# Two kinds of attention scores in the two row halves of TensorE, their matmuls interleaved, the causal mask in two 64-row parts

## The reference

```python
x = x + _L0_attn_ref(_layernorm(x), Wqkv, Wout)
    qkv = z @ Wqkv
    attn = einsum('nhqd,nhkd->nhqk', q, k) * 8 ** -0.5
    attn = softmax(where(causal, attn, -inf))
    out = einsum('nhqk,nhkd->nhqd', attn, v) @ Wout
x = x + _L0_ffn_ref(_layernorm(x), ...)     # 8 experts, two of them per token
x = x + _L1_attn_ref(_layernorm(x), ...)    # rotary, one key and value head for all 16 query heads
x = x + _L1_ffn_ref(_layernorm(x), ...)     # blockwise fp4 quantised, gated
```

## Time and profile before

| | |
|---|---|
| runs | 761.79, 761.80, 763.25 us; median 761.8 |
| profiled execution, first to last instruction | 757.7 us |
| PE matmul busy | 660.7 us (87%), 5007 instructions |
| VectorE busy | 514.1 us (68%) |
| ScalarE busy | 342.2 us (45%) |
| GpSimd busy | 151.8 us (20%) |
| mean granted TensorE clock | 0.965 of full |
| chain that ended last | PE 64%, DVE 25%, issue 5%, ACT 3% |

### The profile page before, as it was taken

One profiled execution on the slowest core, in us unless ns is written; L12 is line 12 of the kernel. 1 busy time (PEld: TensorE's weight loads), 2 busy tenths in 40 slices (PEclk: granted clock), 3 DMA queues, 4 the chain that ended last, 5 costly groups with the idle time before them and its releaser, 6 DMA issues.

```text
span 757.7 us, 13009 instructions
## 1 busy us (share of the span) xinstructions
PE 660.7 (87%) x5007; PEld 464.5 (61%) x5007; DVE 514.1 (68%) x1313; ACT 342.2 (45%) x472; POOL 151.8 (20%) x145
## 2 busy tenths in 40 slices
PE   1478889999989899999999998999989899998664
PEld 0333556565655699898998785775555655555443
DVE  6578776777743536658537467777786778666993
ACT  1110566656575444433444432335546455674221
POOL 5301010100011010010021301302203010345764
PEclk9995999999999999999999999999999999999985
DMA  5405876454320000000000200211211211000000
GB/s 152 126 22 147 173 218 132 85 141 75 66 55 14 1 1 1 1 1 1 1 1 1 63 1 12 75 23 28 83 42 27 65 45 35 25 12 1 14 15 28
DMA packets 29325, 38.07 MB, mean 50 GB/s; under 512 B 3719, under 2 KB 23185, under 8 KB 29265
## 3 DMA queue, kind: packets, MB, share of 16 engines
q1 hardware_dynamic: 29265, 37.25, 20.3%
HBM read 26.33 MB, written 10.88 MB: 49 GB/s over the span
## 4 chain that ended last, share of the span: by engine, by line
PE 64%; DVE 25%; issue 5%; ACT 3%; POOL 1%; DMA 0%; POOLq 0%; DVEq 0%; ACTq 0%
PE ps L989 14%; PE ps L486 9%; PE ps L444 7%; DVE mx L663 6%; PE ps L465 6%; PE ps L979 4%; PE ps L512 3%; PE ps L981 3%; PE ps L980 3%; DVE xn L926 3%; PE ps L447 2%; ACT pT L557 1%; PE ps L494 1%; PE ps L469 1%; DVE x L1063 1%
## 5 line engine op out<-in xcount | busy, mean ns | idle before, releaser
L663 DVE TENSOR_REDUCE mx<-ps 128x1 f32<-128x384 f32 (+3 forms) x352 | 215.5, 637 | 72.5 <-PE ps L447 70.4
L557 ACT ACTIVATE pT<-ps 128x1024 f32<-128x1024 f32 x160 | 162.1, 1023 | 86.9 <-PE ps L469 71.9
L1024 ACT ACTIVATE pT<-ps,b1c 128x512 f32<-128x512 f32 x128 | 87.8, 687 | 129.6 <-PE ps L981 128.7
L989 PEld LDWEIGHTS ps<-w_sb,pT 128*128 128x128 f32 x1024 | 132.2, 191 | 11.8 <-issue 1.3
L989 PE MATMUL ps<-w_sb,pT 128*128 128x128 f32 x1024 | 135.5, 275 | 0.0
L447 PE MATMUL ps<-mask_qk,identb 128*128 128x128 bf16 (+2 forms) x352 | 90.2, 256 | 0.0
L444 PE MATMUL ps<-stA 96*128 96x128 bf16 (+3 forms) x256 | 69.6, 332 | 19.2 <-DVE mx L663 14.3
L486 PE MATMUL ps<-pT,vA 128*32 128x512 f32 (+3 forms) x1024 | 77.9, 439 | 0.7 <-ACT pT L557 0.7
L1063 DVE SCALAR_TENSOR_TENSOR x<-ps,comb,x 128x128 f32<-128x128 f32 x128 | 36.0, 344 | 58.4 <-PE ps L989 58.3
L444 PE MATMUL ps<-kA,stA 96*128 96x128 bf16 (+3 forms) x256 | 63.7, 304 | 12.8 <-DVE mx L663 11.6
L979 PE MATMUL ps<-x_hi,w_hi 128*128 128x512 f32 x128 | 62.9, 491 | 1.2 <-DVE w_lo L1045 1.0
(11 more groups left out here) (232 smaller groups left out, 964.1 us busy)
## 6 DMA issues: line engine op xcount, KB each, us to landing
stA<-stack_scratch SPq DMA_DIRECT2D x48, 192.0 KB, 3.4
stB<-stack_scratch SPq DMA_DIRECT2D x48, 192.0 KB, 4.5
stack_scratch<-part SPq DMA_DIRECT2D x12, 384.0 KB, 3.2
w_sb<-in_L_ffn_W_dram SPq DMA_DIRECT2D x16, 256.0 KB, 5.6
stack_scratch<-part SPq DMA_DIRECT2D x12, 256.0 KB, 3.1
stack_scratch<-part SPq DMA_DIRECT2D x12, 128.0 KB, 3.1
x<-in_L_attn_z_dram SPq DMA_DIRECT2D x4, 256.0 KB, 4.4
out_dram<-x SPq DMA_DIRECT2D x4, 256.0 KB, 2.3
```

The source lines that it names most:

```text
L557: act.activation(dst_, src, ACT.Exp, scale=SCALE).then_inc(a["ex"], 1)
L663: nc.vector.tensor_reduce(mx[:, g % 2, qb, heads[0]:heads[0] + nh], ps[:, S_BANK[n % 2], 0:nh * w].rearrange("p (h k) -> p h k", h=nh), AX ...
L989: last = pe.matmul(ps[:, ST_BANK[1] + m % 2, f * P:(f + 1) * P], hT[:, (m % 2) * FC + c, f * P:(f + 1) * P], w2_sb[:, e, c, :], start=(c = ...
L1024: act.activation(hT[:, (m % 2) * FC + f, :], ps[:, ST_BANK[0] + n % 2, :], ACT.Gelu, bias=b1c[:, e * FC + f:e * FC + f + 1]).then_inc(M["g ...
```

## The change

- S reads partitions 0 to 47, ST partitions 64 to 114 of one stack `st` that replaces `stA` and `stB`. `kA`, the rotary table and the picking columns of layer 1 are made in both places (`KW` = 112 partitions instead of 48), so the key projection has 112 columns.
- No rows are padded, so the clears and the waits on them are gone.
- Each mask matmul (128 rows of identity) becomes two of 64 rows: the first adds the mask's own 64 rows over all 128 columns, the second (`identx`, `mask_x`, which GpSimd makes at the start) adds the other 64 rows to the 64 columns that they touch. S uses the lower half for both, ST the upper.
- Every score and mask matmul is a step of its own, and within a part v the steps of S and ST are merged. Where an attention step is merged with another stage, that merge now counts these finer steps.
- The input loads of the rotary table and the picking columns are six DMAs instead of two.

```diff
+HI = 64
+MR = HI + SR
+KW = HI + SR
+ST_UNITS = [[(j, kb) for kb in (0, 1, 3)] for j in range(HG)] + [[(j, 2) for j in range(HG)]]
+def s_steps(b, g, *units):
+    return [("S", b, g, (u, m)) for u in units for m in range(len(S_UNITS[u][1]) + 2)]
+def st_steps(b, g, u):
+    return [("ST", b, g, (u, m)) for m in range(len(ST_UNITS[u]) + 4)]
...
             for v in range(NV + 1):
-                if s < B:
-                    o.append(("S", s, g, 2 * v))
-                if v < NV and 1 <= s <= B:
-                    o.append(("ST", s - 1, g, v))
-                if v < NV and s < B:
-                    o.append(("S", s, g, 2 * v + 1))
+                plain = s_steps(s, g, *range(2 * v, min(2 * v + 2, NS))) if s < B else []
+                turned_ = st_steps(s - 1, g, v) if v < NV and 1 <= s <= B else []
+                o += merged(plain, turned_)
...
-    o = of("A0", first0[:1]) + setup("QKCOLS") + of("A0", first0[1:2]) + setup("CLEAR")
+    o = of("A0", first0[:1]) + setup("QKCOLS") + of("A0", first0[1:2])
...
-        stA = sb("stA", [KR, 2, 2 * HG, T], BF16)
-        stB = sb("stB", [KR, 2, 2 * HG, T], BF16)
+        st = sb("st", [P, 2, 2 * HG, T], BF16)
...
-                for m, j in enumerate(heads):
-                    h = (g % 2) * HG + j
-                    kk = stA[:, 1, h, :] if layer == 0 else kA[:, b, :]
-                    pe.matmul(ps[:, bank, m * w:(m + 1) * w], stA[:, 0, h, qb * P:w], kk[:, 0:w],
+                if m < nh:
+                    h = (g % 2) * HG + heads[m]
+                    kk = st[0:SR, 1, h, :] if layer == 0 else kA[0:SR, b, :]
+                    pe.matmul(ps[:, bank, m * w:(m + 1) * w], st[0:SR, 0, h, qb * P:w], kk[:, 0:w],
                               start=(m == 0), stop=False)
-                pe.matmul(diagonal, identb[:], mask_qk[:].unsqueeze(1).broadcast_to([P, len(heads), P]),
-                          start=False, stop=True).then_inc(a["sc"], 1)
+                elif m == nh:
+                    pe.matmul(diagonal, identb[0:HI, :], mask_qk[0:HI, :].unsqueeze(1).broadcast_to([HI, nh, P]),
+                              start=False, stop=False)
+                else:
+                    pe.matmul(diagonal[:, :, HI:P], identx[0:HI, :],
+                              mask_x[0:HI, HI:P].unsqueeze(1).broadcast_to([HI, nh, P - HI]),
+                              start=False, stop=True).then_inc(a["sc"], 1)
...
+                    kk = st[HI:MR + 3, 1, h, :] if layer == 0 else kA[HI:MR + 3, b, :]
+                    pe.matmul(o, kk[:, kb * P:(kb + 1) * P], st[HI:MR + 3, 0, h, kb * P:T], start=(at % 512 == 0), stop=False)
...
+                    if not second:
+                        pe.matmul(diagonal, identb[HI:P, :], mask_kq[HI:P, :].unsqueeze(1).broadcast_to([P - HI, nd, P]),
+                                  start=False, stop=False)
+                    else:
+                        last = pe.matmul(diagonal[:, :, 0:HI], identx[HI:P, :],
+                                         mask_x[HI:P, 0:HI].unsqueeze(1).broadcast_to([P - HI, nd, HI]),
+                                         start=False, stop=True)
...
-            if name == "CLEAR":
-                v.memset(stA[:, 1].rearrange("p h t -> p (h t)"), 0.0).then_inc(cleared_a, 1)
...
-            if name == "CLEAR":
-                nc.gpsimd.memset(stB[:].rearrange("p c h t -> p (c h t)"), 0.0).then_inc(cleared_b, 1)
...
-            sp.dma_start(rk[:], rope_k.rearrange("c p t -> p c t")).then_inc(ld_w1, 16)
-            sp.dma_start(pick_sb[:], pick).then_inc(ld_w1, 16)
+            for lo, n in ((0, SR), (SR, HI - SR), (HI, SR)):
+                sp.dma_start(rk[lo:lo + n], rope_k[:, 0:n].rearrange("c p t -> p c t")).then_inc(ld_w1, 16)
+                sp.dma_start(pick_sb[lo:lo + n], pick[0:n]).then_inc(ld_w1, 16)
...
-            nc.vector.memset(stA[:, 0].rearrange("p h t -> p (h t)"), 0.0).then_inc(cleared_a, 1)
...
+            link(nc.gpsimd, nc.gpsimd.memset(identx[:], 0.0))
+            for base in (HI, -HI):
+                link(nc.gpsimd, nc.gpsimd.affine_select(identx[:], identx[:], compare_op=ALU.not_equal, fill=1.0, base=base,
+                                                        pattern=[[-1, P]], channel_multiplier=1))
+            link(nc.gpsimd, nc.gpsimd.memset(mask_x[:], 0.0))
+            link(nc.gpsimd, nc.gpsimd.affine_select(mask_x[:, 0:HI], mask_x[:, 0:HI], compare_op=ALU.is_ge, fill=NEG, base=HI,
+                                                    pattern=[[1, HI]], channel_multiplier=-1))
+            link(nc.gpsimd, nc.gpsimd.affine_select(mask_x[:, HI:P], mask_x[:, HI:P], compare_op=ALU.is_ge, fill=NEG, base=0,
+                                                    pattern=[[-1, HI]], channel_multiplier=1))
```

More of the change, by code:

```diff
@@ L72, with s_last, st_last, merged @@
 NV = HG + 1
+ST_UNITS = [[(j, kb) for kb in (0, 1, 3)] for j in range(HG)] + [[(j, 2) for j in range(HG)]]
[3 more added lines that the diff above has]
+    return [("ST", b, g, (u, m)) for m in range(len(ST_UNITS[u]) + 4)]
+def s_last(step):
+    return step[1] == len(S_UNITS[step[0]][1]) + 1
+def st_last(step):
+    return step[1] == len(ST_UNITS[step[0]]) + 3
+def merged(one, two):
+    at = [((i + 0.5) / len(one), 0, i) for i in range(len(one))] + [((i + 0.5) / len(two), 1, i) for i in range(len(two))]
+    return [(one, two)[w][i] for _, w, i in sorted(at)]
 def attention_order(layer):
@@ L178, in fp4_order @@
     return o + rest(m) + [("DA", n // pairs, n % pairs, 0) for n in (m - 1, m)]
-def merged(one, two):
-    at = [((i + 0.5) / len(one), 0, i) for i in range(len(one))] + [((i + 0.5) / len(two), 1, i) for i in range(len(two))]
-    return [(one, two)[w][i] for _, w, i in sorted(at)]
 def network_order():
@@ L257, in network @@
         mask_kq = sb("mask_kq", [P, P], BF16)
+        identx = sb("identx", [P, P], BF16)
+        mask_x = sb("mask_x", [P, P], BF16)
         ones = sb("ones", [P, P])
@@ L404, in attention_sync @@
             elif name in ("LOADA", "LOADB"):
-                st, ld, used, per = (stA, "loadA", "sc", NS) if name == "LOADA" else (stB, "loadB", "st", NV)
+                lo, ld, used, per = (0, "loadA", "sc", NS) if name == "LOADA" else (HI, "loadB", "st", NV)
                 ws = slice((g % 2) * HG, (g % 2 + 1) * HG)
-                if name == "LOADA" and i == 0 and layer == 0:
-                    sp.wait_ge(cleared_a, 2)
                 if name == "LOADA" and g == 0:
@@ L544, in attention_scalar @@
             if name == "ST":
+                if not st_last(u):
+                    return
+                u = u[0]
                 n = i * NV + u
```

133 lines of the change are left out of this document (68 added, 65 removed).

## The result

The changed kernel takes 795.65 us (median of 4 runs, 793.85 to 797.67) against 761.79 us for the kernel before (4 runs, 760.64 to 763.25): ratio 1.0441, 95% interval 1.0412 to 1.0471. It is 34 us slower, outside the forecast range and with the other sign. Its profiled execution spans 794.5 us (757.7 before), at a mean granted TensorE clock of 0.934 (0.965).

The account below looks back on a forecast made before the run. The prediction took TensorE as the bound, with VectorE 0.9 us behind per group. Its terms summed to -9.4 us on a 757.7 us span, 748.3, plus 4.1 to reach the median: 752.4 us, range 740 to 770.

Parts of the forecast that it names:

- a, head: Start of the kernel: without the clears, normalisations and the first transpose come earlier, -5.6 us.
- b, S alone: Layer 0 with only S: longer masks and more mode changes, partly hidden, +1.2 us (0 to +3).
- Changes of tile: Each change of TensorE's tile size, throughout the kernel, taken as 0.096 us (0 to 0.20).
- c, steps 1 to 3 of layer 0: Layer 0 with S and ST overlapping: twelve groups shorten from 11.27 to about 10.4 us each, -10 us.
- rival 5: TensorE's granted clock drops to 1.2 GHz for 20 us of the steps, 10 us more: 762 us; chance 0.05.
- d, ST alone: Layer 0 with only ST: longer masks and 17 changes, half behind exp, +2.4 us (+1 to +4).
- e, experts with S of layer 1: Expert matmuls land inside S units: 88 added changes and masks, less TensorE idle time, +8 us.
- f, steps 1 to 3 of layer 1: Layer 1 with S and ST overlapping: 0.75 us saved per group over twelve groups, -9 us.
- g, ST alone with fp4: Layer 1's ST alone beside the fp4 stage: masks and 31 changes, a part hidden, +3.6 us.
- Rival 2: The row halves don't overlap, so steps 1 to 3 lengthen in both layers: 796 us; chance 0.10.
- Rival 1: Each of 232 added mode changes costs 0.17 us on the path, not 0.096: 769 us; chance 0.12.
- Rival 3: S waiting for its bank holds up ST, losing half the gain in steps 1 to 3: 762 us; chance 0.10.

Follow-up runs that it names:

- e5: The kernel before, with GpSimd's clear of stB waiting until VectorE's clears of stA are done: 756.02 us, ratio 0.9933.
- e11: The kernel before, with only each mask split into two 64-row matmuls, scores kept at 96 rows: 883.51 us, ratio 1.1605.
- e12: The kernel before, with only the scores cut to 48 and 51 rows, without the zero rows, masks kept single: 884.61 us, ratio 1.1658.
- e4: e2 plus a 64-row, 512-column filler matmul ahead of nine of eleven S units in steps 1 to 3: 776.93 us, ratio 1.0218.
- e8: e4 with the filler also while S is alone in layer 0, and two of them in layer 1: 794.21 us, ratio 1.0438.
- e9: e2 plus a 64-row, 256-column filler matmul ahead of nine of eleven S units in steps 1 to 3: 775.88 us, ratio 1.0197.
- e2: The changed kernel, with S and ST units kept whole where merged with expert or fp4 steps: 784.99 us, ratio 1.0324.
- e3: e2 in the old order, a whole S unit, a whole ST unit, a whole S unit: 781.84 us, ratio 1.0283.
- e10: e9 with its 256-column filler on all 128 rows instead of 64: 793.96 us, ratio 1.0343, with scattered runs.
- e6: The kernel before in its own order, S and ST both in rows 0 to 63, masks in two parts: 856.24 us, ratio 1.1253.
- e1: The kernel before, 96-row stacks and 128-row masks kept, with S and ST matmuls alternating as single steps: 765.11 us, ratio 1.0059.
- e7: e2 with an expert H step and the Y step behind it merged as one block: 793.13 us, ratio 1.0424.

## Why the prediction was wrong, point by point

**a, head (-5.6): right.** Timeline of all engines in the changed kernel:

```profile
7.59 1.11 DVE L938 TENSOR_SCALAR xn<-x,mv,rstd 128x128 f32<-128x128 f32 x4 [1.94 <-POOL rstd L945]
...
8.85 1.09 PE L512 MATMUL ps<-ident,xn 128*128 128x128 f32 x4 [8.85 <-DVE xn L938]
```

The first transpose was at 14.21 and is at 8.85, the first S at 29.2 instead of 34.8: -5.6. e5 shows the clear as the cause, by moving it alone.

**b, S alone (+1.2): too small, +4.8.** TensorE, a score matmul of 512 columns and its mask near the end of this stretch, before and after:

```profile
77.63 0.39 PE L444 MATMUL ps<-stA 96*128 96x512 bf16 x1 [1.07 <-DVE mx L663]
77.85 0.22 PE L447 MATMUL ps<-mask_qk,identb 128*128 128x128 bf16 x1
```

```profile
76.17 0.60 PE L440 MATMUL ps<-st 48*128 48x512 bf16 x1 [0.86 <-DVE mx L680]
76.57 0.31 PE L443 MATMUL ps<-mask_qk,identb 64*128 64x128 bf16 x1
```

0.22 us from start to start before, 0.40 after: after, TensorE is still at half speed here, though the stage row above says 0.99. In both traces the column shows 1.00 up to the first recorded fall, and isn't to be trusted there. The pair of before stands just behind its rise at 76.3: before too had 34.9 of its 44.2 us at half clock, after has all 49.0. The earlier trace rows gave 0.82 for this stage, and I used that only as a warning. e5, with the matmuls of before and 7.4 us more at half clock, takes 1.1 us longer here; at that rate the 14.1 us more are some 2 of the 4.8 (an estimate), and the rest is left to the masks and changes.

**Changes of tile (0.096 us): the price was right (0.10 in e11 and e12).** The Trainium skill (TensorEngine Tiling, Key Properties) says that such a change drains TensorE; the traces agree, with those 0.10 us. What failed is how much of it other work covers. Between the experts the price is the same. TensorE, S and then H in the kernel after:

```profile
482.15 0.32 PE L440 MATMUL ps<-kA,st 48*128 48x384 bf16 x1
482.41 0.50 PE L991 MATMUL ps<-x_hi,w_hi 128*128 128x512 f32 x1
482.75 0.40 PE L992 MATMUL ps<-x_lo,w_hi 128*128 128x512 f32 x1
482.99 0.40 PE L993 MATMUL ps<-x_hi,w_lo 128*128 128x512 f32 x1
483.32 0.23 PE L443 MATMUL ps<-mask_qk,identb 64*128 64x128 bf16 x1
```

384 columns are 0.16 us, and H comes after 0.26; 512 columns of H take 0.24 (L992 to L993), and the mask comes after 0.33: 0.10 on the way out, 0.09 back. H's first pair is 0.34 us apart; but behind a mask it is 0.32 apart in the kernel before as well.

**c, steps 1 to 3 of layer 0 (-10): the failed step, by 20 us (+10.5 - 0.9).** Two things in it were wrong. First, "TensorE bounds, and VectorE stands 0.9 us behind it": e4, with full overlap and at full clock but for 5.1 us, runs groups 4 to 11 in 90.9 us, and groups 12 to 15 of the changed kernel, at full clock by themselves, take 40.5 instead of 41.4. The possible gain was 0.2 us per group and not 0.83. I had kept 2.3 us of VectorE's idle time and let the rest go; in groups 4 to 11 it was 24.8 / 8 = 3.1 before and 3.2 in e4, and only its places changed. So VectorE's loop (reductions, PV, the S behind it, two banks) was nearly as long as TensorE's path, with 8.2 busy and 3.1 idle; a TensorE that finishes sooner waits. Second, the clock, rival 5, which I gave 20 us in one place. After, it is at half for 37.6 us of groups 4 to 11 (27.3 of them recorded). The versions that share this stretch line up: 91.0 us with 5.1 (e4), 91.8 with 6.9 (e8), 94.3 with 16.6 (e9), 97.7 with 28.7 (e2), 97.8 with 31.6 (e3, in the other order), 101.0 with 37.6 (after), some 0.31 us lost per us at half clock; only e10, with its many changes of tile, stands off that line. Most of it is lost in PV (3.4 to 3.9 instead of 2.21 us), where everything waits for TensorE; the idle time ahead of the 384-wide reductions is where it shows:

```profile
L680 DVE TENSOR_REDUCE mx<-ps 128x1 f32<-128x384 f32 x41 | 21.8, 552 | 31.2 <-PE ps L446 31.1
```

**d, ST alone (+2.4): +2.5, by luck.** There are 17 more changes, the masks, and 6.8 us at half clock instead of 3.4. e2, with one change less and 3.4 us at half clock, takes 38.5 us here, e4, the same but for 6.8, takes 40.1: changes and masks cost 0.9 us, the clock 1.6.

**e, experts with S of layer 1 (+8): +11.3, and 2.1 behind it.** 71 more changes were traced, not 88; at 0.10 they are 7.1 us, the two mask parts some 1.7, which makes 8.8; the discount of 2 us for TensorE's idle time was wrong, and 3.4 us at half clock are new. e2 gives +7.2 with 55 changes, e11 +8.7 with 69, e12, without second mask matmuls, +6.1 with 74: 0.08 to 0.13 us per change all in. The 2.1 us behind the stretch are 0.2 in e2. No half clock is recorded in them in either version; 86 matmuls stand there after, 77 in e2 and 66 before, so the finer merge seems to leave more of the last units behind the last H.

**f, steps 1 to 3 of layer 1 (-9): +6.8.** The step that failed is the same as in c. The clock is at half for 37.6 us (3.4 before). The only version with full clock throughout (e8) carries two fillers per unit, which cost time themselves. But the groups 20, 21, 22, 25 and 26 are at full clock before and in e2, and take 59.1 and 57.5 us: 0.3 us per group, where I had taken 0.75.

**g, ST alone with fp4 (+3.6): +5.7, and -0.3 behind it.** 30 more changes at 0.10 and the masks are 4.7, all on the path; the last 1.0 is not explained.

**The rivals.** Rival 2 forecast 796 us, close to what was measured, by a mechanism that is false: the halves overlap to the hundredth of a microsecond (110.27 and 110.28 above; the Trainium skill, TensorEngine Tiling, Tiling Modes, says that different tiles can multiply in parallel, and the trace agrees), and without overlap e6 is at 856, not at 796. Rival 1 (changes cost double) is false in price. Rival 3 (VectorE's pull blocks ST) has little for it: e3, where ST's units stand whole again, has 97.8 us in groups 4 to 11 (97.7 in e2), and at full clock the order is worth 0.16 us per group there and 0.33 in e1. Rival 4, the larger gain, never had room. Rival 5 named the mechanism, with a chance of 0.05 and 20 us of half clock; there were 37.6 in groups 4 to 11 of layer 0 and, by coincidence, 37.6 in layer 1's steps. Its sign followed from the sum; it should have been weighed against a gain that was itself not safe.

**What stays open.** Which property sets the granted clock exactly: rows in use count (e6 and e12 against e11, once each of them is at full clock), but waits seem to as well (e4 against e2), nothing here tells why e11 rises last of all, and repetitions of one stretch scatter (97.7 in e2 and 101.2 in e7 with the same order; one profile of each version). And which wait of VectorE's loop ends last at full clock.

## What to carry to other kernels

Before giving TensorE less to do, check that it bounds: take the other engine's busy and idle time of one period together, and ask of each idle piece what would shorten it. Half-height tiles have a second price beside the 0.10 us at each change of tile: they may cost the granted clock, and then the matmuls that nothing hides (here PV, 3.4 to 3.9 us for 2.21) pay for it. Read the speed from the matmuls' own durations, too, and not from the clock column alone. Zero rows that pad two kinds of matmuls to one tile size were cheap: taking them away from the scores alone cost 124 us (e12).
